# A second tile table made in eight short steps behind every second expert tile instead of six steps behind consecutive tiles

## The reference

```python
K = 2
...
router_logits = (xhat * router_ln_w + router_ln_b) @ router_w + router_b
routing_weights, selected = jax.lax.top_k(router_logits, K)
...
h = jnp.einsum('ebsh,ehi->ebsi', xn, w1) + b1[:, None, None, :]
h = jax.nn.gelu(h, approximate=False)
eo = jnp.einsum('ebsi,eih->ebsh', h, w2) + b2[:, None, None, :]
...
combined = jnp.sum(routing_weights[..., None] * gathered, axis=2)
return _ln_stats(combined) * out_ln_w + out_ln_b
```

## Time and profile before

| | |
|---|---|
| median of 3 runs | 498.81 us (498.32 to 500.5) |
| profiled execution, its own time | 499.39 us |
| its span, first to last instruction | 497.6 us |
| TensorE busy in the span | 436.6 us (88%) |
| VectorE busy | 398.8 us (80%) |
| GpSimd busy | 347.0 us (70%) |
| ScalarE busy | 316.9 us (64%) |

### The profile page before, as it was taken

One profiled execution on the slowest core, in us unless ns is written; L12 is line 12 of the kernel. 1 busy time (PEld: TensorE's weight loads), 2 busy tenths in 40 slices (PEclk: granted clock), 3 DMA queues, 4 the chain that ended last, 5 costly groups with the idle time before them and its releaser, 6 DMA issues.

```text
span 497.6 us, 11499 instructions
## 1 busy us (share of the span) xinstructions
PE 436.6 (88%) x3266; PEld 363.0 (73%) x3266; DVE 398.8 (80%) x1134; ACT 316.9 (64%) x813; POOL 347.0 (70%) x404
## 2 busy tenths in 40 slices
PE   3589999999899899899899766699889999999990
PEld 1366777776677677677677544599889999999980
DVE  2579999999989989989989975467677677786385
ACT  1166778888578678678688645565545555555574
POOL 4675865689979989989987546267567656665632
PEclk9999999999889889889999958599999999999996
DMA  6950000000000000000000050235434322226344
GB/s 152 236 160 0 7 8 5 2 18 19 25 17 19 23 19 19 24 17 19 24 22 14 18 193 23 54 75 175 148 91 105 90 72 69 73 65 229 118 137 125
DMA packets 33934, 33.66 MB, mean 68 GB/s; under 512 B 7037, under 2 KB 27681, under 8 KB 33745
## 3 DMA queue, kind: packets, MB, share of 16 engines
q1 hardware_dynamic: 27600, 22.39, 16.7%
q0 software_dynamic: 4320, 9.22, 5.5%
q10 hardware_dynamic: 1952, 1.32, 1.1%
HBM read 20.43 MB, written 12.48 MB: 66 GB/s over the span
## 4 chain that ended last, share of the span: by engine, by line
PE 49%; POOL 23%; DVE 16%; issue 6%; ACT 4%; DVEq 1%; DMA 0%; ACTq 0%; POOLq 0%
PE sa_ps L1625 12%; POOL xe_dram L388 8%; PE sa_ps L1635 6%; PE bank L1635 6%; PE sa_ps L1403 3%; POOL lgs L422 3%; POOL A_sb L395 3%; PE bank L1616 2%; POOL xn L473 2%; PE bank L1475 2%; POOL kT L445 2%; PE sa_ps L1396 2%; PE bank L1476 2%; PE bank L1600 2%; PE bank L1542 2%
## 5 line engine op out<-in xcount | busy, mean ns | idle before, releaser
L738 ACT ACTIVATE work<-sa_ps,work 128x128 f32<-128x128 f32 x284 | 81.0, 368 | 63.8 <-PE sa_ps L1625 61.9
L483 POOL DMA_INDIRECT y_dram<-work,idxr x71 | 72.4, 1020 | 44.8 <-DVE idxr L1203 32.4
L388 POOL DMA_INDIRECT xe_dram<-xrow,slot x64 | 72.6, 1134 | 24.5 <-issue 14.0
L1625 PE MATMUL sa_ps<-work 128*128 128x128 f32 x568 | 79.4, 284 | 0.0
L1625 PEld LDWEIGHTS sa_ps<-work 128*128 128x128 f32 x568 | 70.5, 195 | 0.2 <-DVE work L1210 0.2
L1403 PE MATMUL sa_ps<-Px,wvT 64*128 64x128 f32 (+1 forms) x288 | 41.4, 338 | 3.8 <-DVE Px L1106 3.7
L1403 PEld LDWEIGHTS sa_ps<-Px,wvT 64*128 64x128 f32 x288 | 33.7, 192 | 13.8 <-DVE Px L1106 9.2
L422 POOL TENSOR_TENSOR lgs<-lgs,rsum 128x256 f32<-128x256 f32 x32 | 30.6, 973 | 18.6 <-DVE rsum L1066 18.6
L1635 PE MATMUL bank<-w2s,work 128*128 x280 | 37.3, 276 | 2.7 <-DVE work L1245 2.7
L1635 PE MATMUL sa_ps<-w2s,work 128*128 x288 | 38.6, 278 | 0.9 <-DVE work L1245 0.6
L395 POOL TENSOR_SCALAR_AFFINE_SELECT A_sb<-A_sb 128x768 f32<-128x768 f32 (+1 forms) x32 | 19.9, 645 | 25.9 <-ACT A_sb L706 25.8
(11 more groups left out here) (280 smaller groups left out, 1119.8 us busy)
## 6 DMA issues: line engine op xcount, KB each, us to landing
work<-xe_dram SPq DMA_DIRECT2D x71, 69.5 KB
work<-in_w SPq DMA_DIRECT2D x1, 2048.0 KB, 9.8
outf<-outf_dram SPq DMA_DIRECT2D x1, 2048.0 KB, 9.8
xrow<-y_dram SPq DMA_DIRECT2D x4, 512.0 KB, 7.4
out<-x_sb SPq DMA_DIRECT2D x7, 256.0 KB, 2.6
y_dram<-work,idxr POOLq DMA_INDIRECT x71, 2.4
modb<-mod_dram SPq DMA_DIRECT2D x16, 64.0 KB, 2.8
xe_dram<-xrow,slot POOLq DMA_INDIRECT x64
```

What stands on the lines that cost most here:

```text
L388: nc.gpsimd.indirect_dma_start(xe_dram, bass.IndirectOffsetOnAxis(slot[:, 4 * batch + column:4 * batch + column + 1], 0), xrow[:, tile, :] ...
L483: nc.gpsimd.indirect_dma_start(y_dram, bass.IndirectOffsetOnAxis(idxr[:, n % RING["scat"]:n % RING["scat"] + 1], 0), y[:, n % RING["scat"] ...
L738: last = nc.scalar.activation(hid[:, n % 2, c, :], up_bank[n % 2][:, c * P:(c + 1) * P], ACT.Gelu, bias=w1c[:, n % 3, FF + c:FF + c + 1])
L1625: last = mm(up_bank[n % 2][:, c * P:(c + 1) * P], w1c[:, n % 3, c * P:(c + 1) * P], xgT[:, n % 3, :], start=True, stop=True)
```

## The change

The six helpers of the second table become one, `late_step(k)`, with k from 0 to 7. Steps are called behind tiles 14, 16, ..., 28. The two reductions have steps of their own. The register of the next tile is loaded ahead of the step and no longer behind it. The last operation of a step is marked and not linked, and the wait for it stands at the head of the next step. `pw` moves from tile 20 to 21 and `gates` from 26 to 27. No operation is added or taken away.

```diff
+        LATE_STEPS = range(14, 30, 2)
...
-            def late_counts():
...
+            def late_step(k):
+
+                n, v = NS - NA, 2 * NE
+                pv = past[:, 0:v * n].rearrange("p (e s) -> p e s", e=v)
+                by_tile = pv.rearrange("p e s -> p s e")
+                if k == 0:
+                    link(nc.vector.tensor_scalar(early_i[:], early_i[:], 7, None, ALU.logical_shift_right))
+                    link(nc.vector.tensor_scalar(count_i[:], count_i[:], 7, None, ALU.logical_shift_right))
+                    nc.vector.tensor_copy(first[:, NE:2 * NE], early_i[:])
+                    nc.vector.tensor_copy(ending[:, 0:NE], early_i[:])
+                    mark(nc.vector.tensor_copy(ending[:, NE:2 * NE], count_i[:]))
+                if k == 1:
+                    link(nc.vector.tensor_tensor(ntile[:], ending[:], first[:, 0:2 * NE], ALU.subtract))
+                    nc.vector.tensor_tensor_scan(tend[:], ones[0:1, 0:2 * NE], ntile[:], 0.0, ALU.mult, ALU.add)
+                    link(nc.vector.scalar_tensor_tensor(out=jump[:], in0=first[:, 1:2 * NE + 1], scalar=float(REGION // P), in1=ending[:], op0=ALU.add, op1=ALU.subtract))
+                    mark(nc.vector.tensor_scalar(jump[:, NE - 1:NE], jump[:, NE - 1:NE], -float(PADROW // P), None, ALU.add))
+                if k == 2:
+                    mark(nc.vector.tensor_tensor(pv, iota_j[:, 0:n].unsqueeze(1).broadcast_to([1, v, n]), tend[:, 0:v].unsqueeze(2).broadcast_to([1, v, n]), ALU.is_ge))
+                if k == 3:
+                    mark(nc.vector.tensor_reduce(exp_f[:, 0:n], by_tile, AX.X, ALU.add))
+                if k == 4:
+                    link(nc.vector.scalar_tensor_tensor(out=exp_f[:, 0:n], in0=past[:, (NE - 1) * n:NE * n], scalar=-float(NE), in1=exp_f[:, 0:n], op0=ALU.mult, op1=ALU.add))
+                    mark(nc.vector.tensor_scalar(exp_i[:, NA:NS], exp_f[:, 0:n], float(NE - 1), None, ALU.min))
+                if k == 5:
+                    mark(nc.vector.tensor_tensor(pv, pv, jump[:, 0:v].unsqueeze(2).broadcast_to([1, v, n]), ALU.mult))
+                if k == 6:
+                    mark(nc.vector.tensor_reduce(row_f[:, 0:n], by_tile, AX.X, ALU.add))
+                if k == 7:
+                    link(nc.vector.scalar_tensor_tensor(out=row_f[:, 0:n], in0=row_f[:, 0:n], scalar=first[:, 0:1], in1=iota_j[:, 0:n], op0=ALU.add, op1=ALU.add))
+                    nc.vector.tensor_scalar(row_i[:, NA:NS], row_f[:, 0:n], float(P), None, ALU.mult).then_inc(S["table_rdy"], 1)
...
-                if n == 14:
-                    late_counts()
-                if n == 15:
-                    late_bins()
-                if n == 16:
-                    tile_bins(NS - NA, 2 * NE)
-                if n == 17:
-                    late_experts()
-                if n == 18:
-                    tile_rows(NS - NA, 2 * NE)
-                if n == 19:
-                    late_rows()
                 if n + 1 < NS:
                     chosen[n + 1] = expert(n + 1)
-                if n == 20:
+                if n in LATE_STEPS:
+                    dve.wait_ge(S["dve_chain"], chain[0])
+                    late_step(LATE_STEPS.index(n))
+                if n == 21:
                     tt(pw[:, AHEAD:NT, 0], top[:, AHEAD:NT, 1], top[:, AHEAD:NT, 0], ALU.subtract).then_inc(S["f_s0"], 1)
-                if n == 26:
+                if n == 27:
                     dve.wait_ge(S["f_s"], 2)
```

## The result

The changed kernel took 497.53 us (median of 18 runs, 495.11 to 500.44) against 500.33 us (18 runs, 498.32 to 503.17). The ratio is 0.9944 with a 95% interval from 0.9922 to 0.9966, so it is faster, by 0.3 to 0.8%. The forecast was 494.65 us in a range from 493.7 to 496.9, from a base of 498.81 us. The measured time lies outside the range, and the ratio of the forecast gain of 4.16 us, 0.9917, lies just outside the interval.

The account below looks back on a forecast made before the run. TensorE bounds the tile loop, except where VectorE makes the second table and 4.16 us are lost. Closing that hole gives 498.81 - 4.16 = 494.65 us, 0.8% faster, with an 8-in-10 range of 493.7 to 496.9.

Parts of the forecast that it names:

- The hole: Tiles 15 to 25: TensorE loses 4.16 us waiting for VectorE's finish while the second table is made; all should go.
- The base: Starting level of the sum: 498.81 us, the median of the runs, 0.58 us below the profiled execution's 499.39.
- VectorE's pace: Tile loop: VectorE alone needs 1.48 us a tile against TensorE's 1.998, leaving 0.52 us for other work.
- the account: Tiles 14 to 29: VectorE's tiles, steps, pw and gates sum to 31.5 us against TensorE's 32.0.
- 0.88, the dearer end: Short steps 1, 4 and 7: between nothing and 0.88 us each, priced at 0.88 like the first step.
- The room: Between down(m) and down(m+2): finish can be 2.6 us late before TensorE waits.
- Register load ahead, no wait for itself: At the table's steps: saves VectorE 6 x 0.6 = 3.7 us; waits at step heads priced at nothing.
- Spreading: Tiles 14 to 29: a step every second tile fits; heaviest pair 3.99 against 4.00 us, worst lag 1.2.
- rival C: Waits for itself cost nothing, crowded steps cost 1.2 us, the rest perhaps loads behind outf: 497.6 us, chance 0.06.
- Who is late next: GpSimd's DMAs and SyncE's tile loads behind outf: close to TensorE's pace, yet nobody waits; last scatter near 381 us.
- D: Load of tile 40: the table comes too late, over 19 us before TensorE waits, so slower; chance 0.03.
- B: Steps' head waits expose the register load, or VectorE and GpSimd hold each other up: 1.7 us remain, 496.4; chance 0.12.

Follow-up runs that it names:

- repeats: The changed kernel measured again twice with no edit: 496.74 us (10 runs), ratio 0.9906, and 496.25 us (6 runs), ratio 0.9890.
- strided work: Changed kernel plus one unused 1.03 us reduction, with the stride of the table's own reductions, at each step's head: loop 110.40 us, ratio 0.9914.
- marks alone: Kernel before, steps in their old places and register load behind them, but each step's last operation marked, its wait heading the next step: loop 111.31 us, ratio 0.9912.
- load ahead alone: Kernel before, steps in their old places, with only the register load moved ahead of the step, last operation still linked: loop 111.52 us, ratio 0.9951.
- spreading alone: Eight steps behind every second tile as in the changed kernel, but last operation linked and register load behind the step: loop 111.18 us, ratio 0.9943.
- strided work, linked: Changed kernel with the added 1.03 us strided reductions, and the last operation of each step but the eighth linked: loop 114.72 us, ratio 0.9996.

## Why the prediction was right or wrong

**The hole.** Right, and near in size. 4.16 us were forecast from ten tiles against 1.998 us a tile, and three profiles of the changed kernel against three of the one before give loops of 109.87 to 109.95 against 113.82 to 114.07, 3.9 to 4.2 us. In the ten tiles themselves it is 3.6 to 3.9 us: they take 20.25 to 20.34 us and not the 20 that the prediction gave, and the rest of the gain lies behind `turn(25)`.

**The base.** This is the step that failed. The sum started at 498.81 us, the median of three runs, and "its own range is 493.7 to 495.7, from the spread of the runs and the choice of the pace". The result rests on 18 runs of the kernel before, of which these three are the first. Their median is 500.33, 1.5 us above that base, and the later measurements had 501.3 to 502.6. The forecast was 2.9 us too low: 1.5 of it is the base and 1.4 the gain, which came out at 2.8 us and not at 4.16. With 4.16 us off 500.33 the forecast would have been 496.2, and its range of 8 in 10, moved up by 1.5, would have ended at 498.4 and held the measured 497.53. The spread has its place ahead of the loop. The starts scatter by 2 to 3 us, the loops of one kernel by 0.25 us or less, and the span ends 34.7 us behind `turn(70)` in all six profiles of the two kernels. Three runs between 498.3 and 500.5 had been read as if they gave the level to within a microsecond.

**The gain of the first measurement.** It was 2.8 us where the loop gains 4.1. The repeats gave ratios of 0.9906 and 0.9890, on the other side of the forecast 0.9917, and their intervals hold it. The start of the loop moves by more between two executions of one program than the missing 1.3 us, but the 2.8 us are a difference of medians of 18 runs each, which vary less than one run. The clock of the runs points the same way. In the first measurement five of the 18 runs of the changed kernel had a mean granted clock of 0.930 or less, with a median of 499.3 us, and nine had 0.936 or 0.937, with 497.2 us. Among the repeats two of 10 and none of 6 were as low. I take the shortfall for this variation. It is shown that the variation exists and that it lies ahead of the changed instructions. That it made this very difference is argued: the clocks of the runs before in the first measurement are not on record, and the start's own shift is open by some tenths of a us.

**VectorE's pace.** The step "VectorE's own pace is 1.48 us a tile" was right as a pace and wrong as a price. It was taken for the engine's time, to which a step's work adds in full, and the engine's own time is 1.06 us. In the account the changed kernel had 31.5 us of VectorE against 32.0, nearly full, and a further 8.2 us of work would then cost 3.5 us and more. They cost 0.5. Over the 16 tiles, from the last `finish` ahead of the steps to that of tile 29's turn, the account has 39.8 us for the kernel with strided work, and the timeline has 33.75 (348.39 to 382.14). With the waits put back it has 38.35 (348.82 to 387.17), so most of the error is the pace and some 1.4 us are the short steps, for which the prediction took "0.88, the dearer end".

The room was wrong too, on the other side. The prediction let `finish` be 2.6 us late before TensorE waits. An estimate of this room: take VectorE's excess, by how much its time from the last `finish` ahead of the steps is above TensorE's 2.0 us a tile where it is worst, and take off what the loop lost against 109.93.

| kernel | VectorE's excess, us | lost by the loop, us | difference |
|---|---|---|---|
| before | 6.15 | 4.14 | 2.0 |
| marks alone | 3.36 | 1.38 | 2.0 |
| load ahead alone | 3.25 | 1.59 | 1.7 |
| spreading alone | 3.24 | 1.25 | 2.0 |
| strided work | 2.19 | 0.47 | 1.7 |
| strided work, linked | 6.86 | 4.79 | 2.1 |

So some 2 us are free, not 2.6. Too much work and too much room cancelled in the run with spreading alone, whose 111.2 us were hit partly by luck. The forecast itself was not hurt, since the changed kernel needs far less than either limit.

**Register load ahead, no wait for itself.** Priced at "6 x 0.6 = 3.7 us" of VectorE's time together (6 x 0.63 is 3.8). In the old places the two edits took 5.3 us off it, since a wait also slows the tile behind it (1.85 us against 1.38 at step 4, above), which the price left out. The runs fit one cause for both edits: a wait that stops the sequencer while the engine has little left in its queue. The stop was 1.5 us long at step 5 of the strided kernel with waits, and with marks alone the wait inside step 1 left 0.69 us of idle time. Either edit alone left 1.4 us or more of the hole, both together none. The waits at the heads of the steps cost nothing that can be seen, as was taken: a step's first operation in the changed kernel has at most 0.29 us of idle time ahead of it, about what a tile without a step has ahead of `finish` (0.23 to 0.25).

**Spreading.** The prediction said that the hole closes since a step with every second tile fits. True, but the old places do as well with the waits gone (109.57 us). By itself the spreading gained 2.9 us (114.07 to 111.18).

**What a wait for itself costs.** Nothing, said rival C. Where a register load or address registers stand behind the wait, the runs say otherwise: 0.6 us for each wait in the kernel with strided work, 0.85 us of idle time in the spread one. Where one operation waits for another with no register work between, the difference is small but there. This is the timeline of VectorE in the kernel before:

```profile
354.07 0.66 DVE L971 TENSOR_TENSOR wmod<-iota_j,tend 1x496 f32<-1x496 f32 x1
354.76 1.03 DVE L972 TENSOR_REDUCE exp_f<-wmod 1x31 f32<-1x496 f32 x1
```

The reduction waits for the compare and starts 0.69 us after it. In the kernel with strided work the compare starts at 359.47 and `finish`, which does not wait for it, at 360.05, 0.58 us after it. So such a wait costs some 0.1 us here, though what stands behind the compare is not the same operation in the two kernels.

**Who is late next.** Nobody, as forecast. The last scatter started at 381.14 where "near 381" was said. `turn(19)` to `turn(22)` had no wait for a load behind `outf`, and the crowded steps do no harm by themselves (109.57 us), so rival C is out. That C's time, 497.6 us, is the measured one to 0.1 us is chance: C had the loop gain 1.2 us, and it gained 4.14. The table was no hindrance to the load of tile 40, so D is out. The sign of B, "idle time of 0.6 us stands ahead of the steps", did not come true.

## What to carry to other kernels

When an engine's operations need registers loaded for each tile, count its sequencer as a resource of its own. Put the register loads ahead of any operation that is waited for, and move a wait on the engine's own result to the place where the result is next read. To test whether the engine or its sequencer sets the pace, add work of known length and see how much of it the tile behind gives back. And a few runs of a kernel give its level to no better than the spread between executions: forecast the difference, and widen the range of the level by that spread.

## What was not expected of the hardware

- A tile of VectorE took 1.48 us in an ordinary place and 1.06 us behind 1.6 us or more of work without a wait, with the same operations. In the changed kernel a single reduction of 1.03 us was enough for the quick sequence (behind `finish` at 362.18 its four operations and the start of `pw` fit into 0.98 us). A single compare of 0.66 us was not: in the tile behind it 0.34 us are idle ahead of the operation at 358.54.
- A reduction of 16 elements to each of 31 results took 1.03 us with a stride of 31 elements inside the sum and 0.66 us with the inputs a broadcast row. Which of the two differences does it was not separated.
- The time from the first instruction to `turn(15)` differed by 2.9 us between two executions of one program. The copies of the first six sequences come the same time apart, within 0.01 us, in both. From there on most intervals between the copies differ, and TensorE's mean granted clock from 112 to 320 us was 0.89 in the one and 0.86 in the other.
